# Turning the regions of a deformable convolution once, in the prologue, and loading them in runs of 4 KB

## The reference

```
x = x + L0(gn(x))     # factorised Fourier terms along rows and columns + a 1x1 mix of the channels
x = x + L1(gn(x))     # a modulated deformable 3x3 convolution
```

## Time and profile before

| | |
|---|---|
| time, median of 3 runs | 2406.02 us (2404.01 to 2407.63) |
| the profiled execution | 2404.01 us, its span 2402.0 us |
| busy share of the span | PE 85%, ACT 74%, DVE 66%, POOL 58% |
| mean granted TensorE clock | 0.968 of full speed |
| DMA | 151 GB/s on average, 363.81 MB |

### The profile page before, as it was taken

The page is one execution under the profiler, slowest core; times in us unless marked ns, Lnnn a source line. Parts: engine busy times, 40 slices in busy tenths (PEclk is TensorE's granted clock), DMA queues, the critical chain, the costliest instruction groups (busy, mean ns, idle before and its releaser), DMA issues.

```text
span 2402.0 us, 126528 instructions
## 1 busy us (share of the span) xinstructions
PE 2034.2 (85%) x50241; PEld 1359.9 (57%) x50241; DVE 1585.7 (66%) x2558; ACT 1787.6 (74%) x3238; POOL 1400.8 (58%) x1803
## 2 busy tenths in 40 slices
PE   8555188988988998898998899889889888988985
PEld 3311056666666666666666666666666666666663
DVE  8699066666666666666666666666666666666663
ACT  0003488888888888888888888888888888888884
POOL 0000166666666666666666666666666666666662
PEclk9699599999999999999999999999999999999997
DMA  8036545556555555655555555565555556556553
GB/s 311 1 140 271 200 115 154 147 149 156 143 149 150 147 151 148 156 143 150 152 147 151 151 154 147 148 156 144 148 152 146 150 148 155 145 149 154 145 151 87
DMA packets 196541, 363.81 MB, mean 151 GB/s; under 512 B 39760, under 2 KB 122480, under 8 KB 192368
## 3 DMA queue, kind: packets, MB, share of 16 engines
q1 hardware_dynamic: 196464, 362.74, 55.7%
HBM read 159.38 MB, written 52.22 MB: 88 GB/s over the span
## 4 chain that ended last, share of the span: by engine, by line
PE 29%; ACT 21%; issue 21%; SPq 5%; DVE 5%; POOL 2%; ACTq 1%; DVEq 1%; DMA 0%; POOLq 0%
PE pV L971 8%; PE pM L996 8%; ACT halves L559 7%; ACT big L585 5%; PE pE L950 5%; SPq L405 4%; PE pR L1016 4%; ACT big L576 4%; PE pM L983 4%; ACT big L598 3%; DVE big L731 2%; DVE big L718 1%; ACT msk L589 1%; POOL halves L478 1%; POOL prod L469 1%
## 5 line engine op out<-in xcount | busy, mean ns | idle before, releaser
L478 POOL TENSOR_TENSOR halves<-prod,halves 128x300 f16<-128x300 f32 x768 | 626.4, 816 | 377.2 <-ACT halves L559 377.1
L731 DVE COPY big<-pE 128x768 f32<-128x768 f32 x768 | 716.9, 933 | 191.3 <-PE pE L950 189.0
L971 PE MATMUL pV<-big 128*32 128x144 f32 x16384 | 816.9, 331 | 4.7 <-issue 1.4
L565 ACT ACTIVATE big<-pE 128x768 f32<-128x768 f32 x768 | 659.7, 859 | 107.7 <-PE pE L950 107.6
L469 POOL TENSOR_TENSOR prod<-big 128x300 f32<-128x300 f32 x768 | 554.2, 722 | 100.8 <-POOL big L493 32.2
L718 DVE STREAM_TRANSPOSE big<-halves 128x384 f32<-128x384 f32 x768 | 440.2, 573 | 197.2 <-POOL halves L478 193.4
L950 PE MATMUL pE<-big,sel_s 32*128 32x64 f16 (+1 forms) x24576 | 411.3, 203 | 174.8 <-DVE big L731 103.6
L950 PEld LDWEIGHTS pE<-big,sel_s 32*128 32x128 f16 x24576 | 329.6, 92 | 386.0 <-issue 373.4
L971 PEld LDWEIGHTS pV<-big 128*32 128x32 f32 x16384 | 482.2, 112 | 102.2 <-issue 6.7
L559 ACT ACTIVATE halves<-prod 128x300 f16<-128x300 f32 x768 | 484.3, 631 | 3.2 <-POOL prod L469 3.0
L493 POOL TENSOR_TENSOR big<-big,msk 128x360 f32<-128x360 f32 x128 | 107.2, 838 | 484.5 <-ACT big L579 484.5
(11 more groups left out here) (72 smaller groups left out, 1175.1 us busy)
## 6 DMA issues: line engine op xcount, KB each, us to landing
v<-big SPq DMA_DIRECT2D x1536, 96.0 KB
win<-xh_scratch SPq DMA_DIRECT2D x128, 544.0 KB, 4.2
big<-xh_scratch SPq DMA_DIRECT2D x384, 136.0 KB, 4.1
xh_scratch<-win SPq DMA_DIRECT2D x32, 544.0 KB, 2.7
big<-in_x SPq DMA_DIRECT2D x16, 1024.0 KB, 16.4
x_scratch<-big SPq DMA_DIRECT2D x16, 1024.0 KB, 3.9
x1r<-x_scratch SPq DMA_DIRECT2D x128, 128.0 KB, 2.1
out<-outs SPq DMA_DIRECT2D x128, 128.0 KB, 1.8
```

What stands on the lines that cost most here:

```text
L478: nc.gpsimd.tensor_tensor(half[:, rn % 2, :, 0:SQ, 1], prod[:, rn % 2, :, :], half[:, rn % 2, :, 0:SQ, 0], ALU.subtract).then_inc(low_done, 1)
L565: nc.scalar.activation(*expanded(1 - q, r, 0), ACT.Copy).then_inc(e_act, 1)
L731: nc.vector.tensor_copy(*expanded(1 - q, r, 1)).then_inc(e_dve, 1)
L971: last = mm(pV[r % 2][b * C:(b + 1) * C, o:o + TAPC], XT[q][:, t * P + b * C:t * P + (b + 1) * C], av[:, b * NT + t, :, :], start=True, st ...
```

## The change

The turning moves to the prologue. After a slot of 8 rows is normalised, POOL cuts it (`cut_strips`), PE transposes it in 9 pieces (`transposes`: 8 pairs of strips and the last one alone), ACT copies them into `xs` (`turned`: two copies of 512 columns and one of 64 x 128), and SP stores `xs` to `xw_scratch`, even strips from partitions 0 to 63 and odd ones from 64 to 127, in two transfers beside that of xh. There a row is one position (row, column in the strip), and holds the channels of the odd strips, then of the even ones. In group 0, PE does this between the mixes of group 1. In a step, `load_regions` of pair N-1 replaces window, strips, transposes and copies: four transfers of 64 partitions x 4 KB into `XT`; the sampling waits for them (`xt_ld`). `strips` takes the place of `v2` in the prologue.

```
-                sp.dma_start(win[:, q, :, :].rearrange("p a b -> p (a b)"),
-                             xh_d[g * P:(g + 1) * P, bass.ds(src, REG_R * PADC)]).then_inc(win_ld[q], 16)
...
+                        sp.wait_ge(xs_done, j * 2 + (g * N_XH + q + 1))
+                        rows = xw_d[bass.ds(j * (2 * XHR * TILE_C) + (g * PADR + TOP + q * XHR) * TILE_C,
+                                            XHR * TILE_C), :]
+                        sp.dma_start(rows[:, 0:ODD * P], xs[XHR * TILE_C:P, q, 0:ODD * P]).then_inc(xw_st[q], 16)
+                        sp.dma_start(rows[:, ODD * P:], xs[0:XHR * TILE_C, q, :]).then_inc(xw_st[q], 16)
...
+            def load_regions(n, q, place):
+
+                g, local = place(n)
+                wait(sp, v_done, (n - 1) * len(VGROUPS))
+                rows = xw_d[bass.ds((local * TILE_R + g * PADR) * TILE_C, REG_R * TILE_C), :]
+                left, right = XT[q][0:REG_R * TILE_C, :], XT[q][REG_R * TILE_C:P, :]
+                sp.dma_start(left[:, 0:ODD * P], rows[:, ODD * P:2 * ODD * P]).then_inc(xt_ld[q], 16)
+                sp.dma_start(left[:, ODD * P:], rows[:, 0:ODD * P]).then_inc(xt_ld[q], 16)
+                sp.dma_start(right[:, 0:ODD * P], rows[:, 0:ODD * P]).then_inc(xt_ld[q], 16)
+                sp.dma_start(right[:, ODD * P:], rows[:, EVEN * P:]).then_inc(xt_ld[q], 16)
...
+            def cut_strips(g, j, q):
+
+                pool.wait_ge(xh_done, j * 2 + (g * N_XH + q + 1))
+                if not (isinstance(j, int) and j == 0 and g == 0):
+                    pool.wait_ge(xs_T, j * 2 + (g * N_XH + q - 1))
+                pool.nop(nofuse=True)
+                nc.gpsimd.tensor_copy(strips[:, q, :, :].rearrange("p s (r x) -> p r s x", r=XHR),
+                                      stg[:, q, :, :].rearrange("p r (s x) -> p r s x", x=TILE_C)) \
+                    .then_inc(strips_done, 1)
...
-                        nc.gpsimd.tensor_copy(strips[:, :, :, :].rearrange("p s r x -> p r s x"),
...
+            def turned(g, j, q):
+
+                act.wait_ge(xs_T, j * 2 + (g * N_XH + q + 1))
+                for k in range(EVEN // 4):
+                    nc.scalar.activation(xs[:, q, k * 512:(k + 1) * 512], pT[q][k][:, :], ACT.Copy)
+                nc.scalar.activation(xs[0:XHR * TILE_C, q, ODD * P:], pT[q][2][0:XHR * TILE_C, 0:P],
+                                     ACT.Copy).then_inc(xs_done, 1)
...
                 with act.Fori(first, N_XH // 2) as j:
                     for q in range(2):
                         act.wait_ge(xh_st[q], (j + g * (N_XH // 2)) * 16)
+                        act.wait_ge(strips_done, j * 2 + (g * N_XH + q - 1))
                         normalize(g, j, q)
+                    for q in range(2):
+                        act.wait_ge(xw_st[q], (j + g * (N_XH // 2)) * 32)
+                        turned(g, j, q)
...
-                        nc.scalar.activation(XT[1 - q][:, k * 512:(k + 1) * 512], pR[:, :],
-                                             ACT.Copy).then_inc(xt_done, 1)
...
+            def transposes(g, j, q):
+
+                pe.wait_ge(strips_done, j * 2 + (g * N_XH + q + 1))
+                if not (isinstance(j, int) and j == 0 and g == 0):
+                    pe.wait_ge(xs_done, j * 2 + (g * N_XH + q - 1))
+                for t in range(EVEN):
+                    pair = strips[:, q, 2 * t:min(2 * t + 2, STRIPS), :].rearrange("p s n -> p (s n)")
+                    rows = P if 2 * t + 1 < STRIPS else XHR * TILE_C
+                    last = nc.tensor.transpose(pT[q][t // 4][0:rows, t % 4 * P:(t % 4 + 1) * P], pair, ident[:, :])
+                last.then_inc(xs_T, 1)
...
-                            pe.wait_ge(xt_done, n * 4 + 4)
+                            pe.wait_ge(xt_ld[q], (n - q) * 32 + 64)
```

More of the change, by code:

```diff
@@ L60 @@
 XHR = 8
+STRIPS = PADC // TILE_C
+EVEN = (STRIPS + 1) // 2
+ODD = STRIPS // 2
 def v_count(act, gi):
@@ L221, in build @@
         pad_st = sem("pad_st")
-        win_ld = [sem(f"win_ld{i}") for i in range(2)]
+        strips_done = sem("strips_done")
+        xs_T = sem("xs_T")
+        xs_done = sem("xs_done")
+        xw_st = [sem(f"xw_st{i}") for i in range(2)]
+        xt_ld = [sem(f"xt_ld{i}") for i in range(2)]
         wino_ld = [sem(f"wino_ld{i}") for i in range(2)]
@@ L452, in _ @@
             last.then_inc(zeroed, 1)
+            def cut_strips(g, j, q):
[6 more added lines that the diff above has]
+                    .then_inc(strips_done, 1)
+            for g in range(g_count):
+                if g == 0:
+                    for q in range(2):
+                        cut_strips(g, 0, q)
+                with pool.Fori(int(g == 0), N_XH // 2) as j:
+                    for q in range(2):
+                        cut_strips(g, j, q)
             def step(N, q, on, place):
@@ L543, in _ @@
                         normalize(g, 0, q)
+                    for q in range(2):
+                        turned(g, 0, q)
                     first = 1
@@ L915, in mix, with mixes @@
                    start=True, stop=True).then_inc(mix_done, 1)
-            for g in range(g_count):
-                first = 0
+            def transposes(g, j, q):
[7 more added lines that the diff above has]
+                last.then_inc(xs_T, 1)
+            MIXES = NXC // N_XH
+            for q in range(2):
+                mix(0, 0, q)
+            with pe.Fori(1, NXC // 2) as j:
+                for q in range(2):
+                    pe.wait_ge(x1_rows, j * 2 + (q - 1))
+                    mix(0, j, q)
+            for g in range(g_count):
+                def mixes(j, g=g):
+                    if g + 1 < g_count:
+                        for h in range(MIXES):
+                            for q in range(2):
+                                pe.wait_ge(x1_rows, j * (2 * MIXES) + ((g + 1) * NXC + 2 * h + q - 1))
+                                mix(g + 1, j * MIXES + h, q)
                 if g == 0:
+                    mixes(0)
                     for q in range(2):
-                        mix(g, 0, q)
-                    first = 1
-                with pe.Fori(first, NXC // 2) as j:
+                        transposes(g, 0, q)
+                with pe.Fori(int(g == 0), N_XH // 2) as j:
+                    mixes(j)
                     for q in range(2):
-                        pe.wait_ge(x1_rows, j * 2 + (g * NXC + q - 1))
-                        mix(g, j, q)
+                        transposes(g, j, q)
             pe.wait_ge(blocks_ld, 16 * NBLOCK)
```

50 lines of the change are left out of this document (16 added, 34 removed).

## The result

| | before | after |
|---|---|---|
| time, median | 2405.02 us | 2507.11 us (2503.5 to 2510.16) |
| ratio | | 1.0428, 95% [1.0402, 1.0453] |
| span of the profiled execution | 2402.0 us | 2508.3 us |
| mean granted TensorE clock | 0.968 | 0.928 |
| first output store | 343.37 us | 412.96 us |

The changed kernel is 102 us slower; 2371 was forecast, and the range ended at 2425. The prologue took 69.6 us more and the 127 steps 36 more.

The account below looks back on a forecast made before the run. No engine alone was taken as the bound, but a path of hand-offs through PE, 16.16 us a step. 2402.0 + 56 (prologue) - 91 (loop) = 2367 us of span, 2371 us of time; range 2330 to 2425.

Parts of the forecast that it names:

- What the removal gives: In the loop, two ACT copies leave the path before round 4: 0.98 us a step, 124 us in all.
- rival 4: Loop path does not shorten by both copies: 2400 us; chance 0.16, shared with a dearer prologue beside late regions.
- The rate of the regions: In a step, the region loads, writing 64 partitions at a time, move 225 GB/s and take 4.66 us.
- When they land: Regions land at A + 16.36, 0.5 us late for the first sampling, every second step; saving 91 us.
- A: The start of a step's first v2 issue on SP, from which the forecast counted its times.
- the issue of the first region load: On SP, behind v2 and three om loads (A + 7.73, then 1.35 us); four region issues follow, 0.45 us each.
- The rest of its step takes 14.48: After a late first sampling at A + 16.4, the step's remainder takes 14.48 us, giving 15.44 us a step.
- the ring: Prologue iteration of normalise, cut, transposes, copies, stores, for two slots on one ACT: about 8.05 us, 8.5 taken.
- the burst of x1: In the prologue, eight 1.05 MB x1 stores of group 1 go out at once: 20.5 us, xh store queues behind.
- the sign: At the prologue's end, the main loop's first load was to go out at 325 to 345 us.
- the bound: In the prologue, PE at half clock makes an iteration 9.05 us; upper prologue cost 68 us with slower stores.
- Rival 2: Regions come much too late at a step's first sampling, below 201 GB/s; kernel slower, 2411 to 2460 us; chance 0.23.

Follow-up runs that it names:

- e2: The changed kernel without region loads from pair 2 on, all pairs sampled from the regions of the first two pairs: 2352.6 us in one run.
- e1: The changed kernel with the four region loads issued ahead of the three om loads in SP's order: 2396.0 us, ratio 0.9957 to the kernel before.
- e12: The changed kernel with four useless 128x384 matmuls, weights 32 wide, ahead of PE's wait for the regions in odd steps: 2445.5 us.

## Why the prediction was wrong

The sum was 2402.0 + 56 - 91 = 2367 us of span. Measured: 2402.0 + 69.6 + 36.4 = 2508.

1. **What the removal gives: right.** "The step becomes 15.18 us": 15.19 with no loads to wait for (e2), 124 us expected and 123 found. The gain lies where it was put, ahead of round 4's expand (the rows of e2); rival 4 is out.
2. **The rate of the regions: right.** 225 GB/s was taken; the landings, 1.14 us apart, make it 230.
3. **When they land: the step that failed first.** "Landed at A + 16.36 ... 0.5 late." Over the odd steps of the loops the last load landed at A + 17.06 (median), 0.70 later than that, and PE started 0.23 behind it, where 0.04 was taken, at A + 17.29, 1.23 late; in the step shown it was 1.84. With the steps written out by hand the wait was 0.77 on average over all steps, where 0.25 was forecast: 66 us. The term that was mis-sized is the issue of the first region load: A + 9.1 by the sum, A + 10.0 in the trace. The `om` loads ahead of it start at A + 8.25, not at A + 7.73, and another 0.4 us passes behind them. From the first issue to the last landing it takes 7.07 us in the kernel after and 7.10 in e1, where the first issue is at A + 8.32; the sum had 7.28. So the rate and the spacing of the four issues (0.64 to 0.75 us, where 0.45 was taken) did not make them late. Nor did the output store, x1r and the next v2, issued into the same queues at A + 14.2, A + 14.8 and A + 15.4: in the even steps, where the output store and v2 come 2 us later, it is 7.01. In the steps written out by hand the longer issue of v2, which the sum did not have, adds to it: ahead of the wait of 3.94 us, v2 took 9.8 us and the first region load went out at A + 11.5.
4. **"The rest of its step takes 14.48": the step that was missing a term.** Behind more than half of the waits PE comes back at half its clock, and the sum had nothing for that. In the kernel after it is 0.47 us a step, 60 us. e12, with the landings left where they were, is 61.6 us faster, some 46 of it clock. The price of half a clock stood in my own rows for the prologue and was asked of nowhere else.
5. **The prologue: the ring was right, its sum was not.** The terms listed for it (0.9, 2.4, 1.3, 1.4, 0.2, 1.3, 1.3) add up to 8.8 us, not to "about 8.05", and 8.9 was measured in group 0 at full clock. DVE would then end 9.9 later instead of 3.8, so that group 1 begins at 251.6 and not at 245.5; it began at 252.0. In group 1 the same terms give 9.3 instead of 8.5, and 9.35 was measured. Added up rightly, the terms put the prologue's cost at some 67 us instead of 56 (an estimate from these terms). Behind the burst of x1 the second iteration came 26.8 us after the first, for 23.1 forecast. The main loop's first load went out at 350.84, not 333.5, and outside the 325 to 345 given as the sign; by the first output store the prologue cost 69.6. Half the clock, for which a whole 1.0 us an iteration was set down as the bound, went with 0.5.
6. **The rivals.** Rival 2 is the case by place and sign, with 0.23, but not by its reason, a rate under 201 GB/s: the regions started late and moved as fast as taken. Even its range, up to 2460, lacked the clock. Its own price for 1.2 us every second step is 0.6 a step, 76 us; that alone with the prologue gives 2402 + 70 - 123 + 76 + 4 = 2429.

The steps add up: 15.19 + 0.77 (the wait) + 0.47 (`om` and first sampling at the lower clock) is 16.43 a step of the 16.44 measured. Of the 141 us between 2367 and 2508, about 66 are waiting, 60 clock and 14 the prologue.

## What to carry to other kernels

When a change moves a load to the place where it lands just in time, work out when its first issue can leave, in the loops and in the steps written out by hand, and ask what the engine does after a short wait: here 1 us of standing still cost up to 1.3 us more in the `om` behind it. Where the time from the first issue to the last landing stays the same (7.1 us here) when the loads are moved in the queue, the issue sets the arrival. Then put the load with the least slack first in its queue, and spread its destination over all partitions; here these two edits and two in the prologue made 2348 of 2507 us. A test for a suspected clock cost is to fill the wait with useless work and leave all else as it is.

## What was unexpected of the hardware

- The `om` behind a wait, most of them of 1 to 2 us, ran at 1.2 GHz in over half the cases (37 of 64); with 0.85 us of the wait filled, in none of those in the loops.
- PE at half its clock cost a ring that it is part of little: 9.35 us an iteration at 0.50, 8.9 at 1.00.
- PE started 0.23 us after the landing it stood waiting for, and 0.04 us after it where it had just come out of other work.
- 40 more matmul instructions, and the weight loads with them, in a loop's body of PE brought 128 packets more on the instruction queue and 22 stalls of up to 8.2 us, in the second group's loop alone; 8 more brought none.
- Four f32 matmuls with weights 128 wide took 2.85 us, four with weights 32 wide in different groups of columns 0.85, for the same 384 columns.
- SP issued twelve v2 loads in 7.57 us inside the loops and in 8.4 to 9.8 in the steps written out by hand.
